# Fourteen instead of twelve of 26 quads by dense products, with counts kept as bytes, in a gated graph network on one core

## What is computed

```python
h = jnp.maximum(_layernorm(x, axis=-1), 0.0)
h = h @ lin_w.T + lin_b
for i in range(3):
    m = h @ weight[i]
    agg = jax.ops.segment_sum(m[src], dst, num_segments=n_nodes)
    h = gru_cell(agg, h, w_ih, w_hh, b_ih, b_hh)
return x + h
```

## Time and profile before

| | |
|---|---|
| median of 3 runs | 4353.29 us (4349.5 to 4356.58) |
| profiled execution | 4358.24 us, span 4356.8 us |
| mean granted TensorE clock | 0.866 of full speed |
| TensorE busy | 3251.4 us (75%) |
| VectorE busy | 2734.1 us (63%) |
| ScalarE busy | 2594.7 us (60%) |
| GpSimd busy | 3195.4 us (73%) |
| read from and written to HBM | 783.68 and 250.48 MB |

### The profile page before, as it was taken

The page is one execution under the profiler, slowest core; times in us unless marked ns, Lnnn a source line. Parts: engine busy times, 40 slices in busy tenths (PEclk is TensorE's granted clock), DMA queues, the critical chain, the costliest instruction groups (busy, mean ns, idle before and its releaser), DMA issues.

```text
span 4356.8 us, 76088 instructions
## 1 busy us (share of the span) xinstructions
PE 3251.4 (75%) x24940; PEld 2780.4 (64%) x24941; DVE 2734.1 (63%) x7740; ACT 2594.7 (60%) x3881; POOL 3195.4 (73%) x3230
## 2 busy tenths in 40 slices
PE   6277777777777678776888788888768787877775
PEld 4155555555555567675777777777767777776774
DVE  7455555565656566665666666666656666666664
ACT  5155655565656566665666666666655665665662
POOL 4777777777777777745777777777667777777776
PEclk8588888888988788888988889998888888998887
DMA  8388888888888987777777777777967777777774
GB/s 269 108 232 225 231 230 230 225 232 228 233 227 232 281 269 252 257 239 229 248 257 250 258 242 264 251 258 247 295 210 237 252 240 250 240 252 238 253 237 133
DMA packets 782766, 1039.46 MB, mean 239 GB/s; under 512 B 91560, under 2 KB 656936, under 8 KB 782376
## 3 DMA queue, kind: packets, MB, share of 16 engines
q1 hardware_dynamic: 515064, 645.79, 45.2%
q0 software_dynamic: 152064, 311.63, 25.2%
q10 hardware_dynamic: 115248, 77.10, 5.6%
HBM read 783.68 MB, written 250.48 MB: 237 GB/s over the span
## 4 chain that ended last, share of the span: by engine, by line
POOL 72%; issue 22%; PE 3%; DMA 1%; DVE 1%; ACT 0%; DVEq 0%; POOLq 0%; ACTq 0%; SPq 0%
POOL ring_region L547 72%; PE psum L839 1%; DMA ring_region<-messages,edge_src 1%; PE psum L737 0%; PE psum L730 0%; PE psum L747 0%; DVE aggT L942 0%; PE psum L794 0%; POOL ring_region L530 0%; DMA messages_region<-in_x 0%; ACT wide_counts L664 0%; DMA messages<-pieces_out 0%; POOL ring_region L528 0%; DVE bn L923 0%; ACT aggT L587 0%
## 5 line engine op out<-in xcount | busy, mean ns | idle before, releaser
L547 POOL DMA_INDIRECT ring_region<-messages,edge_src x3168 | 3141.3, 992 | 1069.8 <-issue 964.7
L664 ACT CAST wide_counts<-messages_region 128x864 fp32r<-128x864 f16 (+1 forms) x1596 | 1540.9, 1031 | 401.4 <-PE psum L839 380.6
L839 PE MATMUL psum<-wide_counts,message_halves 128*128 128x432 f32 x7448 | 1645.0, 380 | 0.0
L839 PEld LDWEIGHTS psum<-wide_counts,message_halves 128*128 128x128 f32 x7448 | 1475.6, 200 | 85.2
L806 PE MATMUL psum<-onehot,ring_region 128*128 128x36 bf16 x9504 | 318.3, 184 | 908.5 <-DMA ring_region<-messages,edge_src 900.9
L806 PEld LDWEIGHTS psum<-onehot,ring_region 128*128 128x128 bf16 x9504 | 286.0, 100 | 1006.7 <-issue 997.7
L687 ACT CAST messages_region<-psum 128x504 f16<-128x504 f32 x1344 | 685.3, 609 | 210.1 <-PE psum L821 184.3
L1255 DVE TENSOR_TENSOR message_halves<-messages_region,message_halves 128x256 fp32r<-128x256 f32 (+1 forms) x1596 | 751.9, 471 | 55.0
L821 PE MATMUL psum<-messages_region 128*128 128x238 bf16 (+2 forms) x5376 | 720.8, 291 | 63.6 <-ACT messages_region L687 45.6
L1253 DVE CAST message_halves<-messages_region 128x256 fp32r<-128x256 f32 (+1 forms) x1596 | 615.2, 385 | 157.0 <-PE psum L839 155.6
L821 PEld LDWEIGHTS psum<-messages_region 128*128 128x128 bf16 x5376 | 517.7, 108 | 249.2 <-issue 57.7
(11 more groups left out here) (103 smaller groups left out, 1671.4 us busy)
## 6 DMA issues: line engine op xcount, KB each, us to landing
messages_region<-counts SPq DMA_DIRECT2D x532, 768.0 KB
counts<-messages_region SPq DMA_DIRECT2D x1344, 128.0 KB
ring_region<-messages,edge_src POOLq DMA_INDIRECT x3168
messages<-pieces_out ACTq DMA_DIRECT2D x98, 192.0 KB
messages_region<-plain SPq DMA_DIRECT2D x21, 896.0 KB, 10.1
temps<-states ACTq DMA_DIRECT2D x98, 128.0 KB
states<-temps ACTq DMA_DIRECT2D x98, 128.0 KB
plain<-temps ACTq DMA_DIRECT2D x98, 128.0 KB
```

Source lines behind the costliest of these rows:

```text
L547: nc.gpsimd.indirect_dma_start(out=rows[:, n % RING, h * QC + c, :], out_offset=None, in_=messages[layer], in_offset=bass.IndirectOffsetOn ...
L664: nc.scalar.copy(wide_counts[:, v % UBUF, :, cols], stage[v % ABUF][:, :, cols]).then_inc(s_wide, 1)
L839: mm = nc.tensor.matmul(psum[:, 6 + kg % 2, 0:DQ * W], halves[:, v % UBUF, b % HB, half * P:(half + 1) * P], wide_counts[:, v % UBUF, :, c ...
```

## The change

- `DQ` goes from 12 to 14: fourteen quads of each superblock are dense, twelve gathered. A mixed superblock has six steps instead of seven; layers 1 and 2 have 96 steps each, layer 0 has 130 + 36. That makes 358 steps and 2864 gathers. A dense product has 504 columns.
- 98 blocks don't divide by six steps, so a step takes seven units (16 or 17 blocks) instead of 14 blocks.
- 224 quads are counted in the same 130 steps: 1568 rounds.
- Counts are bytes from the evacuation on: in the evacuation buffers, in HBM and in the stage buffers. A slab of counts is 459 KB instead of 786 KB; a store of a round is 256 pieces of 256 bytes instead of 512.
- `LEAD` goes from 5 to 4, to match six steps.
- The plan's scratch is moved in `messages_region`, and destinations are loaded straight into `edge_rel`.
- The plan marks equal destinations on one partition of two chunks of a quad as outsiders (then the general order is taken), since a byte holds no more than 255. That is eight more VectorE operations, ahead of the flags.

```diff
-DQ = 12
+DQ = 14
-LEAD = 5
+LEAD = 4
+U8 = mybir.dt.uint8
-    STEP_BLOCKS = 2 * HB
-    assert NB == GSB * STEP_BLOCKS and UBUF * HB == STEP_BLOCKS
+    STEP_UNITS = UN * SLICES // GSB
+    assert STEP_UNITS * GSB == UN * SLICES and STEP_UNITS <= UBUF * UN + 1
+
+    def block_of(unit):
+        return HB * (unit // UN) + UNITS[unit % UN][0]
+
+    def unit_of(d):
+        return UN * (d // HB) + next(j for j, (first, _) in enumerate(UNITS) if first == d % HB)
...
-                now = min(d + STEP_BLOCKS, max(d, end))
+                now = min(block_of(unit_of(d) + STEP_UNITS), max(d, end))
...
-        PB = max(ST0 + ABUF * DQ * SLW * 2, DI0 + DI + 16 * NQ + 4 * RW + 4 * NQ)
+        PB = max(ST0 + ABUF * DQ * SLW, XP + 8 * P + 4 * RW)
...
-        AB = DQ * SLW * 2
-        stage = [half_at(region, ST0 + b * AB, DQ * SLW, F16).rearrange("p (q w) -> p q w", w=SLW)
+        AB = DQ * SLW
+        stage = [byte_at(region, ST0 + b * AB, DQ * SLW, U8).rearrange("p (q w) -> p q w", w=SLW)
                  for b in range(ABUF)]
...
-        dst_i = i32_at(region, DI0, NQ * QC)
-        real_dst = f32_at(region, DI0, NQ * QC)
+        dst_i = edge_rel[:].bitcast(I32)
+        real_dst = f32_at(region, 0, NQ * QC)
...
-        ev = [half_at(region, EV0 + b * 2 * SLW * 2, 2 * SLW, F16).rearrange("p (s w) -> p s w", w=SLW)
+        ev = [byte_at(region, EV0 + b * 2 * SLW, 2 * SLW, U8).rearrange("p (s w) -> p s w", w=SLW)
               for b in range(EVSLOTS)]
...
-            dve.wait_ge(s_out, 1 + QC)
+            ALIKE = ((1, 0), (2, 1), (3, 2), (2, 0))
+            for k, (c, other) in enumerate(ALIKE):
+                nc.vector.tensor_tensor(alike[:, k, :], by_quad[:, :, c], by_quad[:, :, other], ALU.is_equal
+                                        ).then_inc(s_alike, 1)
+            for k, (c, _) in enumerate(ALIKE):
+                dve.wait_ge(s_out, 1 + QC + (QC - 1 if k == QC - 1 else 0))
+                dve.wait_ge(s_alike, len(ALIKE))
+                nc.vector.tensor_tensor(outside_c[:, :, c], outside_c[:, :, c], alike[:, k, :], ALU.max
+                                        ).then_inc(s_out, 1)
+            dve.wait_ge(s_out, 1 + QC + len(ALIKE))
...
-    args["counts"] = nc.dram_tensor("counts", (edges // unit, tiles // (HB * P), P, DQ, SLW), F16, kind="Internal").ap()
+    args["counts"] = nc.dram_tensor("counts", (edges // unit, tiles // (HB * P), P, DQ, SLW), mybir.dt.uint8, kind="Internal").ap()
```

More of the change, by code:

```diff
@@ L211, in gated_graph_layers @@
         DI = NQ * QC * 4
-        DI0 = XP + 8 * P
-        PB = max(ST0 + ABUF * DQ * SLW * 2, DI0 + DI + 16 * NQ + 4 * RW + 4 * NQ)
+        PB = max(ST0 + ABUF * DQ * SLW, XP + 8 * P + 4 * RW)
         region = sb("messages_region", [P, PB // 4])
@@ L255, in half_at, with byte_at @@
             return reg[:, byte // 4:byte // 4 + n // 2].bitcast(dt)
+        def byte_at(reg, byte, n, dt):
+            return reg[:, byte // 4:byte // 4 + n // 4].bitcast(dt)
         hbuf = [temps[:, b * TN:(b + 1) * TN] for b in range(2)] + [third[:]]
@@ L283, in gated_graph_layers @@
         assert R10 + 4 * PTN * 4 <= RING * 8 * MW * 2
-        dst_i = i32_at(region, DI0, NQ * QC)
-        real_dst = f32_at(region, DI0, NQ * QC)
[L287 to L291, removed]
+        dst_i = edge_rel[:].bitcast(I32)
+        real_dst = f32_at(region, 0, NQ * QC)
+        extremes = f32_at(region, DI, 2 * NQ).rearrange("p (k g) -> p k g", k=2)
+        allext = f32_at(region, DI + 8 * NQ, 2 * NQ).rearrange("p (k g) -> p k g", k=2)
+        alike = f32_at(region, DI + 16 * NQ, 4 * NQ).rearrange("p (k g) -> p k g", k=4)
+        group_f = f32_at(region, DI + 32 * NQ, NQ)
+        iota_i = i32_at(region, XP + 8 * P, RW)
         lowest = f32_at(region, ST0, NQ)
@@ L294, in gated_graph_layers @@
         group_i = onehot[:].rearrange("p a b c -> p (a b c)")[:, 0:2 * NQ].bitcast(I32)
[L295 to L299, removed]
+        assert DI + 36 * NQ <= ST0 and ST0 + 4 * NQ <= XP + 8 * P and 4 * NQ <= 3 * 2 * QC * W * 2
         XB = NB * sum(SUBW) * 2
@@ L307, in gated_graph_layers @@
         EV0 = LO0 + 2 * QC * P * 2
-        ev = [half_at(region, EV0 + b * 2 * SLW * 2, 2 * SLW, F16).rearrange("p (s w) -> p s w", w=SLW)
+        ev = [byte_at(region, EV0 + b * 2 * SLW, 2 * SLW, U8).rearrange("p (s w) -> p s w", w=SLW)
               for b in range(EVSLOTS)]
-        assert EV0 + EVSLOTS * 2 * SLW * 2 <= ST0
+        DC = BUILDS * QC
+        KEYS0 = EV0 + EVSLOTS * 2 * SLW
+        keys = f32_at(region, KEYS0, DC)
+        los = f32_at(region, KEYS0 + 4 * DC, DC)
+        split_i = i32_at(region, KEYS0 + 8 * DC, DC)
+        assert KEYS0 % 4 == 0 and KEYS0 + 12 * DC <= ST0
         outside = real_dst
@@ L337, in gated_graph_layers @@
         s_out = sem("outsiders_marked")
+        s_alike = sem("equal_destinations_found")
         s_outsum = sem("outsiders_counted")
@@ L753, in _ @@
             pe.wait_ge(s_r10, PRO * PASSES)
-            pe.wait_ge(s_out, QC + 2)
+            pe.wait_ge(s_out, 2 * QC + 2)
             for c in range(QC):
```

## The result

The changed kernel takes **4100.4 us** (median of 4 runs, 4084.0 to 4104.7) against 4351.4 us for the kernel before on the same chip: a ratio of 0.941 (95% interval 0.939 to 0.943). The forecast was 4031 us, in a range of 3980 to 4110, so the sign and the range held and the middle was 69 us too low. It is the time that rival 2 gave, 4086 and up to 4120, and by the mechanism of rival 2: TensorE takes over.

A forecast was written before the change was run, and what follows sets the result against it. GpSimd's gathers were taken to set the pace in every stage, TensorE having least room. Stages: 124 + 1360 + 373 + 103 + 1017 + 33 + 1003 + 22 = 4035 us, 4031 as median; range 3980 to 4110.

The forecast's parts named there:

- rival 2: TensorE takes over: every superblock's end costs it 3.6 + 2.8 us; 4086 and up to 4120 us in all; 23%.
- rival 1: GpSimd alone stays the bound and TensorE's stands hide, so the whole kernel takes 3990 us; 23%.
- Fewer steps: GpSimd's gathers: one step less per superblock, 72.6 to 62.6 us; -160 us each in layers 1 and 2, -60 in layer 0.
- Products by columns: TensorE's dense products: time grows with columns, 432 to 504, giving 47.0 us of dense work per superblock, 40.3 if columns were free.
- Superblock's end, the stand: TensorE's gate products wait for VectorE's 14 chained additions: 3.6 us per superblock in layers 1 and 2, 5.5 in layer 0.
- The clock after it: TensorE's lower clock after standing at a superblock's end: 0.6 us taken for a 3.6 us stand, 2.8 after 5.5 us.
- Layer 2: TensorE's lateness adds +5 us there, since part is held back and the last five steps have no dense blocks; 1003 us.
- the ring: In layer 2, a ring of four steps holds back some 30 us of TensorE's lateness.
- Pause after layer 1: Between layers 1 and 2: one dense step made dearer, +2 us on 31.
- rival 3: Count stores in 256-byte pieces make DMA set the counting steps; at twice the price per piece +540 us, 4570 us; 6%.
- rival 4: Bytes dear for ScalarE: above +19% widening sets the layers; at twice the price 101 us per superblock, +1450 us; 3%.
- rival 5: The duplicate test sends the kernel into its general order: some 49 x 2.85 us per layer and more; below 1%.

The follow-up runs named there:

- experiment 1: The changed kernel with only the high half of each message in the dense products, so half of TensorE's dense work: 3982 us (one run).
- experiment 3: The changed kernel with nine dense blocks put ahead of the tile's state and gate products in the step after a superblock's end: 3994 us, ratio 0.916.
- experiment 10: The kernel of experiment 3 with eight instead of six mixed superblocks in layer 0, counting in 104 steps: 3854 us, ratio 0.886 to the kernel before.
- experiment 11: The kernel of experiment 3 with nine instead of six mixed superblocks in layer 0, counting in 91 steps: 3876 us, ratio 0.890 to the kernel before.
- experiment 2: The changed kernel with LEAD = 3 instead of 4, tiles one step later against the dense blocks of layers 1 and 2: 4072 us, ratio 0.936.
- experiment 4: The changed kernel with all 14 window positions loaded into VectorE's registers before it waits for the superblock's last dense unit: 4101 us, ratio 0.942.
- experiment 7: The changed kernel with the 14 window positions loaded at the start of VectorE's splits in the step where the superblock ends: 4071 us, ratio 0.935.

## Why the prediction was right and where it was off

- **Bound before** (GpSimd, everywhere): right. Undoing it step by step gives the forecast time when TensorE has room (3982 and 3994 against 3990 of rival 1).
- **Fewer steps**, 62.6 us a superblock on GpSimd: right. 62.3 to 62.4 in the runs that it bounds (experiments 1 and 3), 2864 gathers of 1000 ns.
- **Counting** 1360: right, 1361.7. The rounds hide behind the gathers; experiments 10 and 11 show where their limit is, between 104 and 91 steps.
- **Products by columns**: right, 0.237 us each against 0.2396. TensorE's work was some 58.4 us against the 59.4 forecast.
- **Superblock's end, the stand**: the mechanism was right, down to its 16 waits in layer 1; the size was 4.4 to 4.7 us on average, not 3.6. I had scaled the whole chain (4.56 x 2/12); the additions came to 6.0 us, not 5.3, with 1.6 of it the loads of seven positions. In layer 0 the stands were 5.9 us or longer but for the first, where 5.5 was forecast.
- **The clock after it**: the term that failed. Between 0 and 2.8 us I took 0.6, for a stand of 3.6 us. All ends of layers 1 and 2 but one lost their clock for a while, 2.0 us on average in layer 1 and 2.4 in layer 2. The nearest row, the 2.8 us after 5.5 us of idle time, was much nearer to the price; "no other long idle time left" was a hope and no row. Per superblock of layer 2, 58.4 + 4.4 + 2.4 = 65.2 us stand against 59.4 + 3.6 + 0.6 = 63.6: the stand 0.8 and the clock 1.8 us too small, the work 1.0 too large. That the total lies only 69 us off (1.7%) owes something to this offset, which was luck. Layer 1, where the chain is 0.5 us longer, has a period of 66.3: 16 x (66.3 - 63.6) = 43 us, and 10.5 + 31.3 = 42 are missing in that layer and its pause.
- **Layer 2**: the forecast's +5 did not follow from its own scheme, since 16 x 1.0 us over GpSimd is less than the ring's 30. With the measured 65.2 against 62.4 the scheme gives 16 x 2.8 - 30 = 15 us over 998, and 15 were measured; that the ring's 30 us are right is not shown by that alone.
- **Pause after layer 1**: +2 was forecast by the count of blocks, and TensorE's debt from the layer was left out; it came to 31 us more. The debt of layer 0 I had put into its pause, that of layer 1 into the layer itself, where the ring hides a part of it from GpSimd.
- **Stores of 256 bytes** (rival 3): did not happen; a piece became cheaper, 18.3 instead of 27.9 ns. **Dear bytes** (rival 4): no, the same 910 and 1272 ns. **General order** (rival 5): its 140 us of tiles behind each layer's gathers would show as a pause, and the pauses are 106 and 64 us with dense work in them. **Moved scratch**: the head stayed at 124.7 us.
- **Signs**: waits for rows below 60 us (23.3) and 16 for additions came as said, at 4.7 us instead of 3 to 4. Long waits of GpSimd for TensorE (57 us in 33) were to come only under rival 2, and they came.

## What to carry to other kernels

When one engine is filled up to a few per cent of the bound, look for every place where it must stand for another's serial chain, and price the stand with the slow clock that follows it; then put independent work ahead of the waiting instruction before looking for a shorter chain. A stall that is moved within an in-order engine (experiments 2, 4, 7) returned here in part or as a whole as another's wait, while work that was already there to be done in between (experiment 3) removed it. And busy time alone does not tell a stage's limit where the engines pass one item through each other: with nine dense superblocks the counting stage had outgrown the gathers although its busiest engine was at 84%.

## What the runs showed of the hardware

- TensorE's clock fell with every stand of 4 to 5 us amid otherwise unbroken work (0.53 granted in the 6 us after one of them), and useless products that left 0.75 us of a stand kept it up; 38 times 3.9 us of added work made the kernel 55 us faster.
- Stores in pieces of 256 bytes cost 18.3 ns a piece, in pieces of 512 bytes 27.9: less for a piece, 1.3 times as much for a byte.
  The Trainium skill, "DMA: Bandwidth & Descriptors", Specifications, says that below 512 bytes an engine does a read-modify-write and is off line rate. The dearer byte agrees with being off line rate; what the read-modify-write costs, or whether it took place, no run here shows.
- ScalarE widens uint8 to fp32r at the price of float16, 910 ns for 864 elements a partition.
- Loading seven positions into VectorE's registers keeps it from its work for about 1.6 us, all fourteen for 2.4 to 2.7.
